# A transformer block on one core: q/k projections moved inside each group of attention steps, value products one step later, value copies on GpSimd

## The reference

```python
# attention, 16 heads of 32 features, causal
qkv = jnp.einsum('bsd,ed->bse', x, w_qkv) + b_qkv
scores = jnp.einsum('bhqd,bhkd->bhqk', q, k) / math.sqrt(Hd) + causal
out = jnp.einsum('bhqk,bhkd->bhqd', softmax(scores), v)
x = layernorm(x + (out @ w_out.T + b_out))
# feed-forward, integer weights less 128 times a scale for each row, 2048 hidden features
h = silu(x @ Wg.T) * (x @ Wu.T)
x = layernorm(x + h @ Wd.T)
```

## Time and profile before

| | |
|---|---|
| median of 3 runs | 863.63 us (862.6 to 866.24) |
| the profiled execution: time, span | 862.71 us, 860.9 us |
| PE busy | 790.7 us, 92% of the span |
| DVE, ACT, POOL busy | 469.8, 418.7, 86.9 us |
| groups of batch 1 end (last L1143) | 182.4, 203.4, 226.6, 249.7 us |
| feed-forward begins on PE | 463.1 us |

### The profile page before, as it was taken

How to read it: one execution, slowest core, us unless ns; L and a number is a source line. 1 busy time by engine, 2 the same in 40 slices (tenths; PEclk the granted TensorE clock), 3 DMA queues, 4 the chain that set the end, 5 groups by cost and what they waited for, 6 DMA issues and landing times.

```text
span 860.9 us, 13046 instructions
## 1 busy us (share of the span) xinstructions
PE 790.7 (92%) x4416; PEld 610.3 (71%) x4416; DVE 469.8 (55%) x1054; ACT 418.7 (49%) x962; POOL 86.9 (10%) x71
## 2 busy tenths in 40 slices
PE   6884999999988999999878999999999999999994
PEld 5763677766756677676547888878888788878883
DVE  5344877688746886678655333335322633254336
ACT  5245777667756677577754444442222322232220
POOL 0000002022020411104034000000000000000001
PEclk8897999999998999999769999999999999999998
DMA  7447676558873388664747443210021002000201
GB/s 268 101 66 119 80 127 135 98 87 169 174 123 79 44 171 171 123 123 58 211 157 188 133 120 134 68 49 1 31 69 49 0 24 73 0 1 13 86 0 50
DMA packets 47990, 81.19 MB, mean 94 GB/s; under 512 B 8640, under 2 KB 8640, under 8 KB 47936
## 3 DMA queue, kind: packets, MB, share of 16 engines
q1 hardware_dynamic: 47936, 80.51, 42.6%
HBM read 46.94 MB, written 8.39 MB: 64 GB/s over the span
## 4 chain that ended last, share of the span: by engine, by line
PE 71%; DMA 8%; DVE 6%; issue 6%; ACT 6%; SPq 2%; POOL 0%; DVEq 0%; ACTq 0%; POOLq 0%
PE bank L1258 14%; PE bank L1257 14%; DMA k_stack<-k_hi 7%; PE bank L1263 7%; PE bank L1264 6%; PE bank L1109 5%; PE bank L1132 4%; PE bank L1094 4%; PE bank L1178 4%; PE bank L1243 2%; PE bank L1077 2%; PE bank L1062 2%; PE bank L1064 2%; ACT probs_sb L617 2%; PE bank L1066 2%
## 5 line engine op out<-in xcount | busy, mean ns | idle before, releaser
L617 ACT ACTIVATE probs_sb<-probs_sb,neg_max 128x128 f32<-128x128 f32 (+3 forms) x256 | 142.2, 557 | 68.1 <-DVE neg_max L821 67.6
L821 DVE CUSTOM_DVE_ANT_0 probs_sb<-bank,causal 128x128 f32<-128x128 f32 (+3 forms) x256 | 122.0, 481 | 87.2 <-PE bank L1094 77.0
L946 DVE SCALAR_TENSOR_TENSOR hid<-bank,u_scale,silu 128x512 f32<-128x512 f32 x64 | 48.0, 751 | 181.7 <-PE bank L1258 178.2
L1109 PE MATMUL bank<-ident,probs_sb 128*128 128x128 f32 x640 | 102.3, 285 | 5.6 <-ACT probs_sb L617 4.6
L1263 PE MATMUL bank<-downT,hid_hi 128*128 128x512 f32 x256 | 102.5, 400 | 2.7 <-DVE hid_lo L949 2.7
L1257 PE MATMUL bank<-xT_hi,gateT 128*128 128x512 f32 x256 | 102.5, 401 | 0.0
L1094 PE MATMUL bank<-k_stack,q_stack 96*128 96x128 f32 (+3 forms) x256 | 94.5, 374 | 8.6 <-DVE neg_max L821 6.1
L1264 PE MATMUL bank<-downT,hid_lo 128*128 128x512 f32 x256 | 101.2, 395 | 0.0
L1258 PE MATMUL bank<-xT_lo,gateT 128*128 128x512 f32 x256 | 100.7, 394 | 0.0
L1258 PE MATMUL bank<-xT_lo,upT 128*128 128x512 f32 x256 | 100.4, 392 | 0.0
L1257 PE MATMUL bank<-xT_hi,upT 128*128 128x512 f32 x256 | 100.3, 392 | 0.0
(11 more groups left out here) (96 smaller groups left out, 1311.4 us busy)
## 6 DMA issues: line engine op xcount, KB each, us to landing
q_stack<-q_hi SPq DMA_DIRECT2D x32, 256.0 KB, 7.2
k_stack<-k_hi SPq DMA_DIRECT2D x32, 256.0 KB, 10.3
x_tok<-in_L_attn_x_dram SPq DMA_DIRECT2D x4, 1024.0 KB, 8.3
z_tok<-in_L_attn_x_dram SPq DMA_DIRECT2D x4, 1024.0 KB, 11.6
k_stack<-k_lo SPq DMA_DIRECT2D x16, 256.0 KB, 8.8
q_stack<-q_lo SPq DMA_DIRECT2D x16, 256.0 KB, 10.2
x_tok<-in_L_ffn_gate_w_dram SPq DMA_DIRECT2D x4, 1024.0 KB, 11.8
x_tok<-in_L_ffn_up_w_dram SPq DMA_DIRECT2D x4, 1024.0 KB, 13.1
```

The costliest lines, as they stand in the source:

```text
L617: nc.scalar.activation(probs[qb][:, j, :], probs[qb][:, j, :], ACT.Exp, bias=neg_max[:, qb, j:j + 1], scale=-1.0, accum_out=row_sum[:, qb, ...
L821: nc.vector.tensor_tensor_reduce(out=probs[qb][:, j, :], in0=score[r % 2][:, 0:w], in1=causal[:, S - w:S], scale=-SCALE, scalar=-FLOOR, op ...
L946: nc.vector.scalar_tensor_tensor(out=hid[:, i % 2, :], in0=bank[:, :], scalar=u_scale[:, i:i + 1], in1=silu[:, i % 2, :], op0=ALU.mult, op ...
L1109: last = nc.tensor.transpose(pT[n % 2][:, m * P:(m + 1) * P], probs[qb][:, j, kb * P:(kb + 1) * P], ident[:, :])
```

## The change

1. The fills are spread anew (`filling`). In the loop body, group 0 gets 3 fills in each of the first four steps and 4 in the others, group 1 has 12, 24 and 28 yields with the transposes of x counted in, group 2 is as before, group 3 has none in steps 0 to 3 and then 3 in each. So q and k of group 3 come at steps 4 to 11 where they came at 0 to 5. In batch 0, group 0 gets its fills in steps 10 to 15 only, and group 1 in 4 to 9.
2. The last value job of a batch is done in group 0 of the next one. The transposes of x are fills, too.
3. The value products stand one step later, and the last two portions are done in steps 0 and 1 of the next group. `keep_inverse`, `normalise` and `att_hi` move to steps 1, 3 and 4 (att_hi of group 0 to step 15 of group 1).
4. The copies of the values go from ACT to POOL. The normalisation goes from group 1 to group 2 on POOL; in the last batch it is done by DVE at steps 4 to 7 of group 2.
5. The scans move from steps 9, 11, 5, 7 to 12, 14, 10, 12 and from 2, 4 to 8, 10. The last scan load moves behind the stack of group 3.

```diff
-    PLACE_STEPS = [1, 3, 6, 9]
-    X_STEPS = [8, 10, 12, 14]
-    PRODUCT_STEPS = [4, 6, 11, 13, 15, STEPS]
+    PRODUCT_STEPS = [5, 7, 12, 14, STEPS, STEPS + 1]
     def filling(first, ahead, g):
-        jobs = [("q", g + 2), ("k", g + 2)] if ahead or g + 2 < NG else []
-        if g == 0 and not first:
-            return jobs + [("o", t) for t in range(NT)], [6] * 8 + [3] * 8
-        if g == NG - 2 and ahead:
-            return jobs + [("v", 0), ("v", 1)], [0, 0] + [4] * 6 + [3] * 8
-        if g == NG - 1 and ahead:
-            return jobs + [("v", 2), ("v", 3)], [4] * 8 + [2] * 8
-        return jobs, [3] * 8 + [0] * 8 if jobs else [0] * STEPS
+        qk = [("q", g + 2), ("k", g + 2)] if ahead or g + 2 < NG else []
+        xs = [("x", c) for c in range(ND)]
+        o = [("o", t) for t in range(NT)]
+        if g == 0:
+            if first:
+                return qk, [0] * 10 + [4] * 6
+            return [("v", NT - 1)] + qk + o[:2], [3] * 4 + [4] * 12
+        if g == 1:
+            if first:
+                return qk + xs, [0] * 4 + [4] * 6 + [0] * 2 + [4] * 4
+            return o[2:3] + qk + xs[:2] + o[3:] + xs[2:], [3] * 4 + [4] * 6 + [8] + [4] * 5
+        if not ahead:
+            return [], [0] * STEPS
+        if g == 2:
+            return qk + [("v", 0), ("v", 1)], [0] * 2 + [4] * 6 + [3] * 8
+        return qk + [("v", 2)], [0] * 4 + [3] * 12
...
-    SCAN_STEPS = [2 * STEPS + 9, 2 * STEPS + 11, 3 * STEPS + 5, 3 * STEPS + 7]
-    LATE_SCAN_STEPS = [2, 4]
+    SCAN_STEPS = [2 * STEPS + 12, 2 * STEPS + 14, 3 * STEPS + 10, 3 * STEPS + 12]
+    LATE_SCAN_STEPS = [8, 10]
...
                     if g == 2:
                         load_scan(b, 1)
...
+                    if g == NG - 1:
                         load_scan(b, 2)
...
+            def place_values(b, first, t):
+                if not first:
+                    wait_alone(pool, pv_full, b * NG)
+                jobs = front_jobs if first else jobs_of(b, False, True) if t == NT - 1 else jobs_before(b)
+                wait_alone(pool, pj_drained[jobs.bank("v", t)], jobs.done("v", t))
+                nc.gpsimd.tensor_copy(v_tok[:, t, :], v_next[:, t, :]).then_inc(v_placed, 1)
...
+                    if g == 2 and not first:
+                        root(b - 1, var_done, rstd_done)
+                        if ahead:
+                            wait_alone(pool, rstd_done, b)
+                            for t in range(NT):
+                                apply_norm(t)
...
-                        if s == 1 and g > 0:
+                        if s == 3 and g > 0:
                             normalise(jobs, b, g - 1)
...
+                        if not first and not ahead and g == 2 and 4 <= s < 4 + NT:
+                            apply_norm(b - 1, s - 4, rstd_done, y1_done)
```

More of the change, by code:

```diff
@@ L83, in filled @@
             jobs, counts = filling(first, ahead, g)
-            for n, job in enumerate(jobs):
-                step = next(s for s in range(STEPS) if sum(counts[:s + 1]) >= 3 * ND * (n + 1))
+            need = 0
+            for job in jobs:
+                need += yields(job)
+                step = next(s for s in range(STEPS) if sum(counts[:s + 1]) >= need)
                 over.setdefault(g * STEPS + step + 1, []).append(job)
+            assert need == sum(counts)
         return over
@@ L93, in batch_jobs @@
         for g in range(NG):
[L94 to L97, removed]
+            jobs += filling(first, ahead, g)[0] + [("r", g)]
         return jobs if ahead else jobs + [("f", t) for t in range(NT)]
     IN_FIRST, PER_BATCH = len(batch_jobs(True, True)), len(batch_jobs(False, True))
-    assert IN_FIRST % 2 == 0 and PER_BATCH % 2 == 0
+    assert PER_BATCH % 2 == 0
     class Jobs:
@@ L546, in att_lo, with batch @@
                                         ALU.subtract).then_inc(att_ready, 1)
-            def batch(b, first):
+            def place_values(b, first, t):
[4 more added lines that the diff above has]
+                nc.gpsimd.tensor_copy(v_tok[:, t, :], v_next[:, t, :]).then_inc(v_placed, 1)
+            def batch(b, first, ahead):
                 for g in range(NG):
+                    if g == 0:
+                        for t in range(NT - 1):
+                            place_values(b, first, t)
                     if g > 0:
@@ L553, in batch @@
                         att_lo(b - 1, NG - 1)
-                    if g == 1 and not first:
-                        for t in range(NT):
-                            apply_norm(b - 1, t)
+                    if g == 0:
+                        place_values(b, first, NT - 1)
+                    if g == 2 and not first:
[4 more added lines that the diff above has]
+                                apply_norm(t)
                     if g == NG - 1:
@@ L562, in batch @@
                         last.then_inc(res_ready, 1)
-            batch(0, True)
-            with pool.Fori(1, B) as b:
-                batch(b, False)
+            batch(0, True, True)
+            with pool.Fori(1, B - 1) as b:
+                batch(b, False, True)
+            batch(B - 1, False, False)
             att_lo(B - 1, NG - 1)
@@ L618, in exponential @@
                                      scale=-1.0, accum_out=row_sum[:, qb, j:j + 1]).then_inc(exp_done, 1)
[L620 to L626, removed]
             def keep_inverse(jobs, b, g):
@@ L679, in batch @@
                                 qk_hi(jobs, b, kind, n)
+                            if kind == "x":
+                                x_hi(jobs, n)
                         if r == 0:
@@ L909, in batch @@
                             inverse_sum(b, v)
-                        if s == 1 and g > 0:
+                        if s == 3 and g > 0:
                             normalise(jobs, b, g - 1)
-                        if s == 1 and g == 0 and not first:
+                        if s == 3 and g == 0 and not first:
                             normalise(jobs_before(b), b - 1, NG - 1)
@@ L1161, in _ @@
                     pass
-            work = project(front_jobs, None, 1)
+            work = chain(project(front_jobs, None, "q", 1), project(front_jobs, None, "k", 1))
             for r in range(PER_HALF):
@@ L1187, in batch @@
                     spread, counts = filling(first, ahead, g)
[L1188 to L1190 removed]
+                    work = chain(*(project(jobs, jobs if (kind, n) == ("q", NG) else None, kind, n) if kind in "qk" else
+                                   transpose_x(jobs, b + 1, n) if kind == "x" else
+                                   project_out(jobs, "o", b - 1, n) if kind == "o" else
+                                   project_values(jobs, n) for kind, n in spread))
                     for s in range(STEPS):
```

93 lines of the change are left out of this document (46 added, 47 removed).

## The result

The changed kernel takes 903.4 us, the median of 4 runs (901.16 to 905.94), beside 864.58 us for the kernel before (862.6 to 866.24) on the same chip. The ratio is 1.0451, with a 95% interval of 1.041 to 1.0492: slower, and by far more than forecast. Its profiled execution took 905.94 us with a span of 904.0. It is the slowest of its four runs, so accounts by the two traces (43.1 us between the spans) lie some 4 us above what the medians show (38.8).

What follows compares the result with a forecast made beforehand. Attention was taken as mostly PE-bound, its groups nearly full, with DMA waits in batch 0. Terms 4.9 + 0 + 0.9 + 2.5 + 2.5 - 2 + 2.7 = +11.5 on 862.7 gave 874.2, so 875 us as median; range 860 to 883.

Steps and rivals of the forecast that it cites:

- the full groups: Batches 1 and 2: gains and new waits cancel, 0 each (-3 to +2); batch 3's groups 0 and 1, +0.9 us.
- The bank at step 4: Groups 0 and 1: PE's job waits for normalise to drain the inverse sums' bank, 0.6 to 0.7 us lost in each.
- The bank at step 10: Group 1: the second x block waits for the bank that k_lo drains, about 1 us.
- Batch 0: Group 2's stack starts 8.3 us later, PE waits 7 us in group 1; +4.9 us net (+2 to +8).
- The branch: Loop's branch back: DVE's stall grows about 2 us as the stack starts later; +2.5 us (1.4 to 6).
- Batch 3's normalisation: Group 2 of batch 3: DVE waits some 2.6 us for the root and does four normalisations; +2.5 us (0 to +5).
- The end: End of the attention: later scan load delays DVE's first output, PE waits about 2.1 us; +2.7 us (+0.6 to +7).
- POOL's copies: Group 0's value copies on POOL: taken at 1.3 us each, hidden before the values are wanted.
- (1): Full groups win what they can, new waits absorbed, -3 in each of batches 1 to 3: 857 us; chance 0.16.
- (2): Batch 0 costs its forecast 4.9 us, the rest cancels: some 865 us; chance 0.17.
- (3): The branch and the end both reach their upper bounds, 3.5 and 4.3 us more: 883 us; chance 0.17.
- (4): q_hi waits stay because stacks are as late as q and k, 0.9 us per batch 1 to 3: 878; no separate chance.

Runs made afterwards that it cites:

- the normalise edit: Changed kernel with normalise at step 2, ahead of the reciprocal, instead of step 3 behind reciprocal and eviction: 892.5 us, 10.9 less.
- its reverse: The written-out kernel with the old fills and later products, with normalise moved back from step 2 to step 3: 879.3 us, 26.0 more.
- both edits: Changed kernel with normalise at step 2 and the x blocks moved apart to steps 12 to 15 of group 1: 881.0 us, 22.4 less.
- the old fills: Changed kernel, batches 1 and 2 written out, normalise at step 2, fills back in their former groups, only group 0's spread differently: 853.3 us, ratio 0.9858.
- the edit: Changed kernel with the fills of batch 0's groups 0 and 1 where the kernel before had them: 896.9 us, 6.5 less.
- the kernel before written out: Kernel before the change with batches 1 and 2 written out by a Python loop, so no engine branches back: 853.7 us, ratio 0.9844.

## Why the prediction was wrong

The direction was right, and 875 with a range to 883 was not: the span grew by 43.1 us (the medians by 38.8) for 11.5 forecast. The step that failed is the one on the full groups. It said that 0.6 to 0.7 is lost in each of groups 0 and 1 at step 4, about 1 us at step 10, and that the sum for batches 1 and 2 is nothing, with bounds of -3 and +2. They measured +13.2 and +14.8, of which 3.5 is the branch. The same step gave +0.9 for groups 0 and 1 of batch 3, which measured +11.0 (28.0 and 34.4 for 30.4 and 21.0). Together that is some 35 of the 43.1 us.

1. **The bank at step 4.** I saw the mechanism, and named it as what decides, but took 0.6 to 0.7 where it is 1.9 to 2.0. The time of DVE's eviction came from group 2, which has no fills in its first two steps: PE issues the score of step 2 there 1.4 us into the group, but 4.0 us into group 1 of the changed kernel, and DVE's chain of maximum, reciprocal, maximum and eviction starts only behind that score. In groups 0 and 1 it ends at 8.5 us with `normalise`, not 6.5, while PE is there at 6.6. Shown by the normalise edit and its reverse.
2. **The bank at step 10.** I priced one wait at 1 us. There are three, 1.9, 1.4 and 1.0: a block of x takes PE only four short transposes, and DVE drains a job one step behind it, so that the job two places on finds its bank undrained. Shown by moving the x blocks.
3. **The clock.** This term was left out altogether. I counted 2 us of slow clock behind the 7 us wait of batch 0 and nothing behind the short ones, although showed what 0.50 costs. Of two waits of 1.9 and 1.4 us, 1.2 us apart, the second had 6.8 us at 0.51 begin within it, and one of 1.93 was followed by 3.4 us. The four waits in group 1 of batch 1 (1.9, 1.9, 1.4, 1.0) and what the clock took there are 6.2 + 4.6 = 10.8 of the 15.1 us that it grew.
4. **The rest, some 4 us, is for the most part work that was moved.** Group 1 has 24 fills more than before (two output jobs), group 0 12 fewer and group 3 12 fewer. With both edits batch 1 takes 99.0 us, 2.3 over before; with the old fills it takes 97.6. Group 3's 21.2 us, worked out for batch 0 and the same in batch 1, measured 21.5.
5. **Batch 0** was forecast by its own steps: group 0 to end at 85.4 (85.6), PE to wait 7 us in group 1 (5.5), group 1 to end at 114.1 (116.5). +4.9 forecast, +7.4 measured; by the edit, 6.5 of it is the fills' place.
6. **The branch**: gap of 10 to 12 forecast, 11.3 measured; group 0 of batch 2 +2.5 forecast, +3.5 measured. The Trainium skill, "DMA: Bandwidth & Descriptors", section "Queues, rings and completion order", has the queues served in turn, by which the gap would not have followed the stack. It did, both ways: 8.8, 11.3, 8.7. Every run with the branch and the changed kernel's group 3 shows 11.3. The packet of instructions moves as the transfers end, 11.0 to 12.3 us after the stack's last DMA, whether DVE branches 2.0 or 5.8 us after it; when it was asked for is not in the trace.
7. **Batch 3's normalisation** cost nothing that can be seen. DVE waited 2.6 us for POOL's root as forecast, but group 2 took 20.4 us for 20.9, where I had +2.5 and -1. Group 3 took 16.4 for 21.9, 5.5 less where I had 1 less: PE is idle for 2.1 us in it, for 5.6 before, and at 0.79 for 0.69. This is not the new fills' doing, for with the old fills it takes 17.0, in the kernel before written out 20.7; the later products and the later scans are in both, and no run tells them apart. **The end**, from group 3 to the feed-forward, took 17.9 us for 13.8, +4.1 where I had +2.7: PE waited the 2.1 us in the output jobs, and of the rest 1.7 is a stretch of 3.4 us at 0.50, which I had not counted. Group 3 and the end of the changed kernel:

```profile
473.40:489.80 16.40, 14.29 (x103) 8.70 (x100) 11.90 (x25) 13.37 (x34) 6.24 (x5) 0.79 0.36 130
489.80:507.70 17.90, 14.34 (x67) 10.31 (x65) 8.26 (x18) 3.71 (x6) 1.81 (x3) 0.90 0.85 222
```

8. **POOL's copies** were priced at 1.3 us each and take 0.62, as long as on ACT. They are hidden at either price, as the return to ACT shows.

Rivals: (1), that the new waits are absorbed, named the right place, step 4, and the wrong sign. (2) and (3) fell by their size. (4), that the waits of q_hi stay, is out: behind batch 0 ACT waits for no stack.

What stays open: why the clock falls behind a 1.93 us wait in batch 1 and not behind the same wait in batch 2. No run here varied that alone. Open, too, is why PE is busy longer in the kernel with the old fills and the later products. The fastest two kernels, the one before written out (853.7) and this one (853.3), are level and both written out: no part of the change is shown to gain anything over the whole kernel.

## What to carry to other kernels

When work shares a bank with a short drain, write down for each user when the drain is done and when the matrix engine arrives, from a stretch that has the same load, and put the drain ahead of any long instruction of its engine: standing behind a reciprocal of 1.75 us, a maximum and an eviction it cost 10.9 us of 903 in one kernel and 26 of 879 in another. Price a short stall of the matrix engine at up to twice its length, as measured here for stalls of 1.4 to 2 us, for the clock may fall behind it. In a kernel whose groups are full, redistributing can win only the idle rest; look first for what stands outside them, here one branch that cost 11 us of 864.

## What the runs showed of the hardware that was not expected

Waits of 1.4 to 2 us of a PE that was otherwise full brought, not each time, 3.4 to 6.8 us at 1.2 GHz (batch 1 of the changed kernel; the same 1.93 us wait in batch 2 did not). The restart of DVE behind a branch back came 13.3 to 14.5 us after the issue of the last DMA of a stack in flight, in three kernels with three gaps (8.8, 11.3, 8.7), and 1.9 us behind the end of the first packet of instructions in each; without the branch 0.4 us remained. A 128x512 float32 copy took 0.62 us on POOL, and a two-operand one of the same size 1.28.
